# Graph edge stage on Trainium2: gathers wait for their own indices, run eight steps ahead and are spread between the scatters

## The chip, the cores and the metric

The kernel runs on one core of one Trainium2 chip. The metric is the device time of one execution in microseconds (us); the median of three runs of the kernel before is 3663.58 us (3653.1 to 3665.04).

## What is computed

```python
def _L0_gnn_ref(m, row, col, vals):            # m = layernorm(x): 50000 x 256; 25000 edges
    H = m.astype(jnp.float16)
    v = vals.astype(jnp.float16)
    msgs = H[col] * v[:, None]                 # col = dst (sorted), row = src
    return jax.ops.segment_sum(msgs, row, num_segments=N).astype(m.dtype)

x = x + _L0_gnn_ref(_layernorm(x, axis=-1), src, dst, edge_weight)
x = x + _L0_ffn_ref(_layernorm(x, axis=-1)[None], gate_w, gate_b, w1, b1, w2, b2)[0]
```

The second line is a mixture of 8 experts with a capacity limit: each of the 50000 rows is normalised, sent to the expert with the largest gate value, and passed through two matrix products there. Only the first line is touched by the change.

## The kernel before

The program has three stages, each a block of its own with a barrier at its end, so that no engine starts a stage before all have ended the last one: the **edge stage** (`edge_and_constants`), which fills a table `agg` in HBM with the sums over edges; **routing** (`route_tokens`), which reads x and `agg` in 49 steps of 1024 rows, and scatters the rows to their experts' queues; and the **experts** (`run_experts`).

The edge stage takes the 25000 edges in S = 25 steps of 1024 (`STEP`), each as G = 8 columns of 128. Step s goes like this:

- SP (`load`, L153) loads the step's indices: `dst_col`, `src_col` and `w_col` of 4 KB each, and `src_row`, the 1024 source numbers broadcast to 128 partitions (512 KB). All four raise one semaphore, `idx_loaded`, and stand in one of `INPUTS` = 3 buffers. `edge_done` counts the steps whose indices and rows are used up; SP waits for it before it writes into a buffer again.
- POOL (`gather`, L186) waits for `idx_loaded`, and for `edge_done` where its buffer of `rows` was in use, and issues 8 indirect DMAs, each of which fetches 128 rows of x into `rows` (L195).
- DVE (`body`, L296) takes the statistics of the 8 gathered tiles (`bn_stats`, L305), ACT the square root (`std`, L258) and the normalised rows (L265), DVE the masks of equal source numbers (`same`, L292; `earlier`, L334) and the weighted messages (L340). PE counts the earlier edges with the same source (L366) and sums the messages of equal sources (`ps_sum`, L376). DVE then writes `target` (L349), the row of `agg` that each sum goes to, and raises `edge_done`; ACT copies the sums out of PSUM in four parts (`sums`, L275, raising `sums_out`). ACT works in order: the square root of step s + 1 stands behind the four copies of step s.
- POOL (`scatter`, L200) waits for `edge_done` and `sums_out` of the step, and for `added` of the scatter before it, since two accumulating scatters must not be in flight together, and issues 8 accumulating indirect DMAs into `agg` (L212). `sums` and `target` have `HOLD` = 6 buffers.

POOL's order is written out by hand: gathers of steps 0 to 5, scatter(0), and from there gather(s + 5), scatter(s) by turns, in a hardware loop in the middle; the last five scatters stand alone. A number behind scatter or gather is that of its step in this text.

Before scatter(0), `agg` has to be zero. ACT issues 25 writes of 1 MB from `zeros` (L250, `zero`): 2 at once, the rest one at a time at six places of each step's body, raising `agg_zeroed`. The rest of SP's work in the stage, two loads of expert weights, follows its last index load.

Of the kernel before, what the change touches and what calls it, by code (L numbers as in the profile page):

```python
# [27 lines left out]
I32 = mybir.dt.int32  # L28
U8 = mybir.dt.uint8

P = 128
G = 8
STEP = G * P
# [23 lines left out]
HOLD = 6  # L57
INPUTS = 3
# [14 lines left out]
def edge_and_constants(nc, ctx, t):  # L73
# [22 lines left out]
    dst_col = sb("dst_col", [P, INPUTS, G], I32)  # L96
# [27 lines left out]
    agg_zeroed = sem("agg_zeroed")  # L124
    idx_loaded = [sem(f"idx_loaded{r}") for r in range(INPUTS)]
# [16 lines left out]
    AHEAD = HOLD - 1  # L142
# [6 lines left out]
    with nc.Block() as block:  # L149

        @block.sync
        def _(sp):
            def load(i, r):  # L153
                s, h = HOLD * i + r, r % INPUTS

                if not (isinstance(i, int) and s < INPUTS):
                    sp.wait_ge(edge_done, s + 1 - INPUTS)
                b = base_of(i, r)
                sp.dma_start(dst_col[:, h, :], row_view(dst[bass.ds(b, STEP)])).then_inc(idx_loaded[h], 16)
                sp.dma_start(src_col[:, h, :], row_view(src[bass.ds(b, STEP)])).then_inc(idx_loaded[h], 16)  # L160
                sp.dma_start(w_col[:, h, :], row_view(weight[bass.ds(b, STEP)])).then_inc(idx_loaded[h], 16)
                sp.dma_start(src_row[:, h, :], src[bass.ds(b, STEP)].partition_broadcast(P))\
                    .then_inc(idx_loaded[h], 16)
# [11 lines left out]
        def _(pool):  # L175
# [10 lines left out]
            def gather(i, r):  # L186
                s, h = HOLD * i + r, r % INPUTS

                pool.wait_ge(idx_loaded[h], 64 * (turn(i, r) + 1))
                pool.nop(nofuse=True)  # L190
                if not (isinstance(i, int) and s < INPUTS):
                    pool.wait_ge(edge_done, s + 1 - INPUTS)
                    pool.nop(nofuse=True)
                for c in range(G):
                    pool.indirect_dma_start(  # L195
                        out=rows[:, h, c, :], out_offset=None, in_=x[:, :],
                        in_offset=bass.IndirectOffsetOnAxis(ap=dst_col[:, h, c:c + 1], axis=0),
                    ).then_inc(gathered[h], 16)

            def scatter(i, r):  # L200
                s = HOLD * i + r
# [4 lines left out]
                if isinstance(i, int) and s == 0:  # L206
                    pool.wait_ge(agg_zeroed, 16 * ZEROS)
                else:
                    pool.wait_ge(added[r - 1], 16 * G * (i + 1 if r else i))
                    pool.nop(nofuse=True)  # L210
# [5 lines left out]

            for r in range(AHEAD):
                gather(0, r)
            gather(0, AHEAD)
            scatter(0, 0)  # L220
            for r in range(1, HOLD):
                gather(1, r - 1)
                scatter(0, r)
            with pool.Fori(1, S // HOLD - 1) as i:
                gather(i, AHEAD)
                scatter(i, 0)
                for r in range(1, HOLD):
                    gather(i + 1, r - 1)
                    scatter(i, r)
            n = S // HOLD - 1  # L230
            gather(n, AHEAD)
            scatter(n, 0)
            gather(n + 1, 0)
            for r in range(1, HOLD):
                scatter(n, r)
            scatter(n + 1, 0)
            for r in range(HOLD):
                pool.wait_ge(added[r], 16 * G * (n + (2 if r == 0 else 1)))

        @block.scalar  # L240
        def _(act):
# [9 lines left out]

            zero(0, 2 + max(0, ZEROS - AHEAD * (BANKS + 2)))

# [26 lines left out]
        def _(v):  # L280
# [15 lines left out]
            def body(i, r):  # L296
                s, h, q = HOLD * i + r, r % 2, r % INPUTS
                n = Count(s * PER + SET)
                v.wait_ge(idx_loaded[q], 64 * (turn(i, r) + 1))
# [883 lines left out]
```

## Time and profile before

| | before |
|---|---|
| median of 3 runs | 3663.58 us (3653.1 to 3665.04) |
| profiled execution: span, first to last instruction | 3533.8 us |
| the same execution's own time | not shown; the median is 129.8 us above the span |
| edge stage | 0 to about 697.5 us, barrier to 706 |
| routing | 706 to about 1310 us |
| experts | about 1310 to 3533.8 us |
| POOL busy in 105 to 600 us | 402.1 of 495 us |
| DVE, PE, ACT busy there | 260.8, 221.4, 130.2 us |
| DMA queues' share of 16 engines there | 0.45 |

A busy share counts an instruction's own time. A DMA instruction on POOL is busy while its descriptors are written; the transfer lands later, and a row on landing tells how much later. Between two instructions a profile row gives the idle time and what ended it; "issue" is idle time in which the engine waited for nothing that is shown. A wait for several semaphores is put down to the one that came last by the profile.

### The profile page before, as it was taken

Reading aid. Unit: us, or ns where it says so; the run is one execution under the profiler, and the core shown is the slowest. Engines: PE = TensorE matmul, PEld = TensorE weight load, DVE = VectorE, ACT = ScalarE, POOL = GpSimd, SP = SyncE. Lnnn points to the kernel's source line nnn. Section 1 sums busy time; section 2 is a strip of 40 time slices with the busy share of each in tenths; the row PEclk is TensorE's granted clock in tenths of the full one; section 3 lists DMA queues with packets and bytes.
Section 4 is the critical chain, followed back from the end, with each engine's and each line's share of the span. In section 5 each row is a group of like instructions: output and inputs, shape, how many; then the busy total and the mean of one; then the engine's idle time right before and its main releaser. Section 6 shows DMA issues by size and latency. Waiting matters only on the chain.

```text
span 3533.8 us, 60004 instructions
## 1 busy us (share of the span) xinstructions
PE 2919.1 (83%) x18982; PEld 2664.8 (75%) x18983; DVE 2291.9 (65%) x5804; ACT 1564.2 (44%) x2603; POOL 1796.0 (51%) x1195
## 2 busy tenths in 40 slices
PE   4544434078888876999999999999999999999998
PEld 3433434078888875988989988888988989998987
DVE  6655455077777764676676676676676676667666
ACT  2322222045555543554454555454555444454453
POOL 4788887647777773334343333434333433334332
PEclk8766666555555557999999999999999999999999
DMA  9544444399999963111111111111111121111110
GB/s 344 135 86 76 90 76 87 29 290 302 306 307 292 281 201 111 49 52 62 55 54 50 49 45 51 62 53 59 49 44 50 42 68 41 49 55 32 49 46 26
DMA packets 303467, 371.32 MB, mean 105 GB/s; under 512 B 35431, under 2 KB 263812, under 8 KB 300080
## 3 DMA queue, kind: packets, MB, share of 16 engines
q1 hardware_dynamic: 221504, 199.21, 19.2%
q0 software_dynamic: 78304, 145.23, 15.4%
q10 hardware_dynamic: 3600, 26.22, 1.8%
q8 instruction: 22, 0.36, 0.0%
q14 instruction: 37, 0.30, 0.0%
HBM read 184.33 MB, written 195.85 MB: 108 GB/s over the span
## 4 chain that ended last, share of the span: by engine, by line
PE 55%; DVE 3%; issue 2%; DVEq 1%; DMA 0%; SPq 0%; POOL 0%; ACT 0%; POOLq 0%; ACTq 0%
PE u_Y L1125 29%; PE u_H L1114 24%; PE u_T L1099 2%; DVE y L1058 1%; DVE yo L1077 1%; DVE yo L1074 0%; DVE y L1063 0%; DVE hn L1029 0%; DVE low L1068 0%; DVE hlo L1047 0%; DVE yo L1072 0%; DMA u_pay<-slots 0%; DMA slots<-blank 0%; DVEq L882 0%; DVEq L881 0%
## 5 line engine op out<-in xcount | busy, mean ns | idle before, releaser
L967 POOL DMA_INDIRECT out_x<-yo,u_token x360 | 712.3, 1979 | 1330.5 <-DVE yo L1079 1243.7
L1125 PE MATMUL u_Y<-whi,hhi 128*128 128x256 f32 x2880 | 816.0, 283 | 2.2 <-DVE hlo L1047 2.2
L999 ACT ACTIVATE hm<-u_H,b1e 128x512 f32<-128x512 f32 x720 | 496.3, 689 | 712.3 <-PE u_H L1114 684.0
L1125 PE MATMUL u_Y<-wlo,hhi 128*128 128x256 f32 x2880 | 807.2, 280 | 0.0
L1125 PE MATMUL u_Y<-whi,hlo 128*128 128x256 f32 x2880 | 806.2, 280 | 0.0
L1114 PE MATMUL u_H<-xhi,whi 128*128 128x512 f32 x1440 | 570.8, 396 | 3.1 <-DVE xlo L1036 2.5
L1114 PE MATMUL u_H<-xlo,whi 128*128 128x512 f32 x1440 | 570.3, 396 | 0.0
L1114 PE MATMUL u_H<-xhi,wlo 128*128 128x512 f32 x1440 | 570.0, 396 | 0.0
L1125 PEld LDWEIGHTS u_Y<-whi,hhi 128*128 128x128 f32 x2880 | 545.1, 189 | 2.4 <-DVE hlo L1047 2.4
L1125 PEld LDWEIGHTS u_Y<-wlo,hhi 128*128 128x128 f32 x2880 | 545.0, 189 | 0.0
L1125 PEld LDWEIGHTS u_Y<-whi,hlo 128*128 128x128 f32 x2880 | 544.3, 189 | 0.0
L534 POOL DMA_INDIRECT slots<-pay,slot_i x392 | 457.5, 1167 | 163.7 <-issue 122.5
L1058 DVE TENSOR_TENSOR y<-u_Y,b2e 128x256 f32<-128x256 f32 x360 | 127.7, 418 | 614.1 <-PE u_Y L1125 614.1
L1003 ACT ACTIVATE hhi<-hm 128x512 fp32r<-128x512 f32 x720 | 456.0, 633 | 22.9
L1047 DVE TENSOR_TENSOR hlo<-hm,hhi 128x512 fp32r<-128x512 f32 x720 | 452.7, 702 | 2.9 <-ACT hhi L1003 2.9
L212 POOL DMA_INDIRECT agg<-sums,target x200 | 328.5, 1642 | 79.2 <-issue 58.8
L599 PEld LDWEIGHTS ps_L<-gw,hT 128*128 128x128 f32 x1568 | 350.3, 332 | 0.1
L614 PE MATMUL ps_T<-ident,h 128*128 128x128 f32 x784 | 208.7, 431 | 167.3 <-ACT h L565 167.3
L599 PE MATMUL ps_L<-gw,hT 128*128 128x8 f32 x1568 | 342.4, 352 | 0.0
L1114 PEld LDWEIGHTS u_H<-xhi,whi 128*128 128x128 f32 x1440 | 271.0, 188 | 65.9 <-issue 4.1
L1114 PEld LDWEIGHTS u_H<-xhi,wlo 128*128 128x128 f32 x1440 | 270.9, 188 | 65.5
L1114 PEld LDWEIGHTS u_H<-xlo,whi 128*128 128x128 f32 x1440 | 271.0, 188 | 61.5
(127 smaller groups left out, 3757.4 us busy)
## 6 DMA issues: line engine op xcount, KB each, us to landing
xt<-in_x SPq DMA_DIRECT2D x49, 1024.0 KB
out_x<-pay SPq DMA_DIRECT2D x49, 1024.0 KB, 6.0
u_pay<-slots SPq DMA_DIRECT2D x91, 534.0 KB, 3.9
agg<-zeros ACTq DMA_DIRECT2D x25, 1024.0 KB, 10.9
at<-agg SPq DMA_DIRECT2D x49, 512.0 KB
raw<-in_L_ffn_w POOLq DMA_DIRECT2D x14, 1024.0 KB, 6.9
src_row<-in_src SPq DMA_DIRECT2D x25, 512.0 KB
slots<-pay,slot_i POOLq DMA_INDIRECT x392
```

The lines of the kernel that those rows point to most:

```text
L212: pool.indirect_dma_start(out=agg[:, :], out_offset=bass.IndirectOffsetOnAxis(ap=target[:, r, c:c + 1], axis=0), in_=sums[:, r, c, :], in_ ...
L534: pool.indirect_dma_start(out=slots[:, :], out_offset=bass.IndirectOffsetOnAxis(ap=slot_i[:, r, g:g + 1], axis=0), in_=pay[:, r, g, :], in ...
L599: last = pe.matmul(logits[:, g, :], hT[:, g * KD + kd, :], gw[:, kd, :], start=(kd == 0), stop=(kd == KD - 1))
L614: last = pe.transpose(ps_T[:, n, :], h[:, q, g, kd * P:(kd + 1) * P], ident[:])
L967: pool.indirect_dma_start(out=out[:, :], out_offset=bass.IndirectOffsetOnAxis(ap=token[:, s:s + 1], axis=0), in_=yo[:, s, :], in_offset=No ...
L999: act.activation(hm[:, f, :], ps_H[:, f % 2, :], ACT.Relu, bias=b1e[:, f:f + 1])\
L1003: act.activation(hhi[:, f, :], hm[:, f, :], ACT.Copy).then_inc(hhi_ready, 1)
L1047: v.tensor_tensor(hlo[:, f, :], hm[:, f, :], hhi[:, f, :].bitcast(F32), ALU.subtract)\
L1058: last = v.tensor_tensor(y[:, s, :], ps_Y[:, s, 0:D], b2e[:], ALU.add)
L1099: last = pe.transpose(ps_T[:, k, s * P:(s + 1) * P], hn[:, s, k * P:(k + 1) * P], ident[:])
L1114: last = pe.matmul(ps_H[:, f % 2, :], w1_at(w, buf, k, f), a[:, k, :], start=(j == 0), stop=(j == len(passes) - 1))
L1125: last = pe.matmul(ps_Y[:, s, 0:D], a[:, f, cols], w2_at(w, buf, f), start=(f == 0 and j == 0), stop=(f == KF - 1 and j == 2))
```

## The change

- **Index loads apart.** `dst_col` gets `HOLD` buffers and a semaphore of its own, `dst_loaded`. SP issues step s's `dst_col` load before it waits for `edge_done`, and the other three after. A gather waits for `dst_loaded` alone and, from step `INPUTS` on, for `edge_done`; DVE waits for the other three loads.
- **Buffers.** `INPUTS` goes from 3 to 4 and `HOLD` from 6 to 8. A gather of step s now needs `edge_done` of step s - 4 instead of s - 3.
- **Order on POOL.** 64 gathers (steps 0 to 7) stand ahead of scatter(0), instead of 48. The other 136 are dealt out evenly, 5 or 6 ahead of each of the scatters 1 to 24. The hardware loop is gone; all is straight code. The other engines keep their loop, with a body of 8 steps instead of 6.
- **Zeroing.** ACT issues 12 of the 25 writes at once, and the rest at the same six places of each step.

```diff
-HOLD = 6
-INPUTS = 3
+HOLD = 8
+INPUTS = 4
...
-    dst_col = sb("dst_col", [P, INPUTS, G], I32)
+    dst_col = sb("dst_col", [P, HOLD, G], I32)
...
             def load(i, r):
                 s, h = HOLD * i + r, r % INPUTS
+                b = base_of(i, r)
+                sp.dma_start(dst_col[:, r, :], row_view(dst[bass.ds(b, STEP)])).then_inc(dst_loaded[r], 16)
                 if not (isinstance(i, int) and s < INPUTS):
                     sp.wait_ge(edge_done, s + 1 - INPUTS)
-                b = base_of(i, r)
-                sp.dma_start(dst_col[:, h, :], row_view(dst[bass.ds(b, STEP)])).then_inc(idx_loaded[h], 16)
                 sp.dma_start(src_col[:, h, :], row_view(src[bass.ds(b, STEP)])).then_inc(idx_loaded[h], 16)
...
+            def gather(s, c):
+                r, h = s % HOLD, s % INPUTS
+                if c == 0:
+                    pool.wait_ge(dst_loaded[r], 16 * (s // HOLD + 1))
+                    pool.nop(nofuse=True)
+                    if s >= INPUTS:
+
+                        pool.wait_ge(edge_done, s + 1 - INPUTS)
+                        pool.nop(nofuse=True)
+                pool.indirect_dma_start(
+                    out=rows[:, h, c, :], out_offset=None, in_=x[:, :],
+                    in_offset=bass.IndirectOffsetOnAxis(ap=dst_col[:, r, c:c + 1], axis=0),
+                ).then_inc(gathered[h], 16)
...
+            HEAD = HOLD * G
+            SPREAD = S * G - HEAD
+            for n in range(HEAD):
+                gather(n // G, n % G)
+            scatter(0)
+            for s in range(1, S):
+
+                for n in range(HEAD + SPREAD * (s - 1) // (S - 1), HEAD + SPREAD * s // (S - 1)):
+                    gather(n // G, n % G)
+                scatter(s)
...
-            zero(0, 2 + max(0, ZEROS - AHEAD * (BANKS + 2)))
+            zero(0, ZEROS // 2)
...
-                v.wait_ge(idx_loaded[q], 64 * (turn(i, r) + 1))
+                v.wait_ge(idx_loaded[q], 48 * (turn(i, r) + 1))
```

**POOL at the start of the stage.** Each `L195` row with a wait is the first gather of a step, the `x7` behind it the other seven; `L212` is a scatter. Before, from the gathers of step 4 on:

```order
L195 DMA rows<-in_x,dst_col 128x256 [waits idx_loaded1,edge_done]
L195 DMA rows<-in_x,dst_col 128x256 x7
L195 DMA rows<-in_x,dst_col 128x256 [waits idx_loaded2,edge_done]
L195 DMA rows<-in_x,dst_col 128x256 x7
L212 DMA agg<-sums,target 51200x256 [waits edge_done,sums_out,agg_zeroed]
L212 DMA agg<-sums,target 51200x256 x7
```

and with the change, from step 4 on:

```order
L195 DMA rows<-in_x,dst_col 128x256 [waits dst_loaded4,edge_done]
L195 DMA rows<-in_x,dst_col 128x256 x7
L195 DMA rows<-in_x,dst_col 128x256 [waits dst_loaded5,edge_done]
L195 DMA rows<-in_x,dst_col 128x256 x7
L195 DMA rows<-in_x,dst_col 128x256 [waits dst_loaded6,edge_done]
L195 DMA rows<-in_x,dst_col 128x256 x7
L195 DMA rows<-in_x,dst_col 128x256 [waits dst_loaded7,edge_done]
L195 DMA rows<-in_x,dst_col 128x256 x7
L212 DMA agg<-sums,target 51200x256 [waits edge_done,sums_out,agg_zeroed]
L212 DMA agg<-sums,target 51200x256 x7
```

The gathers of steps 6 and 7 now stand ahead of scatter(0), and gather(7) waits until step 3 has used its buffers.

**POOL at the end of the stage.** Before, the last gathers and what follows them (gather(24), scatter(19), then scatter(20) to (24); the row that waits for `added5` at the top is scatter(18)):

```order
L212 DMA agg<-sums,target 51200x256 [waits edge_done,sums_out,added5]
L212 DMA agg<-sums,target 51200x256 x7
L195 DMA rows<-in_x,dst_col 128x256 [waits idx_loaded0,edge_done]
L195 DMA rows<-in_x,dst_col 128x256 x7
L212 DMA agg<-sums,target 51200x256 [waits edge_done,sums_out,added0]
L212 DMA agg<-sums,target 51200x256 x7
L212 DMA agg<-sums,target 51200x256 [waits edge_done,sums_out,added1]
L212 DMA agg<-sums,target 51200x256 x7
```

and with the change, from the gathers ahead of scatter(22), the row that waits for `added5`:

```order
L195 DMA rows<-in_x,dst_col 128x256
L195 DMA rows<-in_x,dst_col 128x256 [waits dst_loaded7,edge_done]
L195 DMA rows<-in_x,dst_col 128x256 x3
L212 DMA agg<-sums,target 51200x256 [waits edge_done,sums_out,added5]
L212 DMA agg<-sums,target 51200x256 x7
L195 DMA rows<-in_x,dst_col 128x256 x4
L195 DMA rows<-in_x,dst_col 128x256 [waits dst_loaded0,edge_done]
L195 DMA rows<-in_x,dst_col 128x256
L212 DMA agg<-sums,target 51200x256 [waits edge_done,sums_out,added6]
L212 DMA agg<-sums,target 51200x256 x7
L195 DMA rows<-in_x,dst_col 128x256 x6
L212 DMA agg<-sums,target 51200x256 [waits edge_done,sums_out,added7]
```

The first gather in this list is the last one of step 22; the row with `dst_loaded7` begins step 23, the one with `dst_loaded0` step 24. The last gathers of a step have moved from five scatters ahead of its own scatter to directly ahead of it.

## Rows read from the trace of the kernel before

**Rows 1.** Routing stage: busy us and count of each engine, clock, DMA share, GB/s.

```profile
core 0: us, PE busy (x) PEld busy (x) DVE busy (x) ACT busy (x) POOL busy (x), PEclk, DMA share, GB/s
...
706.00:1310.00 604.00, 521.93 (x2779) 502.92 (x2779) 445.31 (x1758) 322.98 (x637) 444.52 (x383) 0.50 0.94 289
```

**Rows 2.** POOL's groups, 0 to 720 us (busy us, mean ns, idle before).

```profile
L212 POOL DMA_INDIRECT agg<-sums,target x200 | 328.5, 1642 | 79.2 <-issue 58.8 <-DMA agg<-sums,target 12.8 <-DMA agg<-zeros 7.3
L195 POOL DMA_INDIRECT rows<-in_x,dst_col x200 | 193.3, 966 | 94.4 <-issue 59.4 <-DMA src_row<-in_src 26.2 <-DVE target L349 8.4
```

**Rows 3.** POOL (start us, us, what): first gathers of steps 0, 3, 4, 5; scatter(0), (1).

```profile
7.80 1.14 POOL L195 DMA_INDIRECT rows<-in_x,dst_col  x1 [5.70 <-DMA src_row<-in_src]
...
43.21 0.94 POOL L195 DMA_INDIRECT rows<-in_x,dst_col  x1 [4.84 <-DMA src_row<-in_src]
...
68.83 0.94 POOL L195 DMA_INDIRECT rows<-in_x,dst_col  x1 [15.70 <-DMA src_row<-in_src]
...
87.50 0.94 POOL L195 DMA_INDIRECT rows<-in_x,dst_col  x1 [8.45 <-DVE target L349]
...
104.76 1.63 POOL L212 DMA_INDIRECT agg<-sums,target  x1 [7.29 <-DMA agg<-zeros]
...
130.65 1.61 POOL L212 DMA_INDIRECT agg<-sums,target  x1 [0.30 <-issue]
```

**Rows 4.** Timeline of SP, first load as steps 0, 3 end; one src_row.

```profile
34.97 0.33 SPq L159 DMA_DIRECT2D dst_col<-in_dst  x1
...
73.47 1.13 SPq L162 DMA_DIRECT2D src_row<-in_src  x1
86.83 0.35 SPq L159 DMA_DIRECT2D dst_col<-in_dst  x1
```

**Rows 5.** Statistics of step 0, its last copy of sums, standard deviation of step 1.

```profile
20.90 2.71 DVE L305 BATCH_NORM_STATS2 e_stats<-rows 128x6 f32<-128x256 f32 x8 [13.71 <-DMA rows<-in_x,dst_col]
...
43.51 0.60 ACT L275 ACTIVATE sums<-ps_sum 128x512 f16<-128x512 f32 x1 [1.15 <-PE ps_sum L376]
...
44.01 0.29 ACT L258 ACTIVATE e_std<-e_mv,eps 128x8 f32<-128x8 f32 x1
```

**Rows 6.** Landing of gathers, 40 to 56, 66 to 105, 105 to 300 us.

```profile
DMA to landing us min/median/max: 7.3/7.6/7.8
...
DMA to landing us min/median/max: 7.2/8.1/8.6
...
DMA to landing us min/median/max: 2.7/3.0/4.6
```

**Rows 7.** DMA, 40 to 100 us; then 0 to 105; last, zeroing in 80 to 105.

```profile
DMA packets 5526, 24.83 MB, mean 414 GB/s; under 512 B 1987, under 2 KB 1987, under 8 KB 3019
...
DMA packets 10074, 36.35 MB, mean 346 GB/s; under 512 B 4435, under 2 KB 4435, under 8 KB 6867
...
agg<-zeros ACTq DMA_DIRECT2D x3, 1024.0 KB, 13.0
```

**Rows 8.** Timeline of one step amid the stage, from its last gather.

```profile
181.05 0.95 POOL L195 DMA_INDIRECT rows<-in_x,dst_col  x1 [0.30 <-issue]
...
206.96 0.60 ACT L275 ACTIVATE sums<-ps_sum 128x512 f16<-128x512 f32 x1 [1.15 <-PE ps_sum L376]
```

**Rows 9.** Timeline of the end: last gather, scatter (19), last copy of sums, last scatter.

```profile
595.59 0.94 POOL L195 DMA_INDIRECT rows<-in_x,dst_col  x1 [0.30 <-issue]
...
596.84 1.62 POOL L212 DMA_INDIRECT agg<-sums,target  x1 [0.30 <-issue]
...
620.79 0.60 ACT L275 ACTIVATE sums<-ps_sum 128x512 f16<-128x512 f32 x1 [1.15 <-PE ps_sum L376]
...
695.93 1.55 POOL L212 DMA_INDIRECT agg<-sums,target  x1 [0.30 <-issue]
```

**Rows 10.** Scatters, 100 to 600 us beside DVE; then 612 to 698 alone.

```profile
L212 POOL DMA_INDIRECT agg<-sums,target x154 | 256.7, 1667 | 53.9 <-issue 46.3 <-DMA agg<-zeros 7.3 <-ACT sums L275 0.3
...
L212 POOL DMA_INDIRECT agg<-sums,target x41 | 63.4, 1547 | 23.8 <-DMA agg<-sums,target 12.8 <-issue 11.0
```

More of the change, by code:

```diff
@@ L124, in edge_and_constants @@
     agg_zeroed = sem("agg_zeroed")
+    dst_loaded = [sem(f"dst_loaded{r}") for r in range(HOLD)]
     idx_loaded = [sem(f"idx_loaded{r}") for r in range(INPUTS)]
@@ L141, in edge_and_constants @@
     PER_BANK = G // BANKS
-    AHEAD = HOLD - 1
     turn = lambda i, r: (HOLD // INPUTS) * i + r // INPUTS
@@ L184, in _, with scatter @@
                                pattern=[[-1, P]], channel_multiplier=1).then_inc(pool_set, 1)
[L186 to L192, printed above, removed]
-                    pool.nop(nofuse=True)
[L194 to L201, printed above, removed]
+            def gather(s, c):
+                r, h = s % HOLD, s % INPUTS
+                if c == 0:
+                    pool.wait_ge(dst_loaded[r], 16 * (s // HOLD + 1))
+                    pool.nop(nofuse=True)
+                    if s >= INPUTS:
[5 more added lines that the diff above has]
+                ).then_inc(gathered[h], 16)
+            def scatter(s):
+                r = s % HOLD
                 pool.wait_ge(edge_done, s + 1)
@@ L205, in scatter @@
                 pool.nop(nofuse=True)
-                if isinstance(i, int) and s == 0:
+                if s == 0:
                     pool.wait_ge(agg_zeroed, 16 * ZEROS)
                 else:
-                    pool.wait_ge(added[r - 1], 16 * G * (i + 1 if r else i))
+                    pool.wait_ge(added[(s - 1) % HOLD], 16 * G * ((s - 1) // HOLD + 1))
                     pool.nop(nofuse=True)
@@ L215, in scatter @@
                     ).then_inc(added[r], 16)
[L217 to L236, printed above, removed]
+            HEAD = HOLD * G
[7 more added lines that the diff above has]
+                scatter(s)
             for r in range(HOLD):
-                pool.wait_ge(added[r], 16 * G * (n + (2 if r == 0 else 1)))
+                pool.wait_ge(added[r], 16 * G * (S // HOLD + (r < S % HOLD)))
         @block.scalar
```

## The prediction, made before the changed kernel was run

> **What bounds the kernel now.** I read the stages first (table above): the change touches the edge stage alone, and a barrier ends it, so what that stage gains or loses is what the kernel gains or loses. In the middle of the stage POOL is the bound. Its groups [rows 2] show 200 scatters at 1.642 us and 200 gathers at 0.966 us, and about 0.30 us of "issue" behind each (118.2 us over 400, which ends when nothing but the next issue was due). A gather so costs 1.27 us. A turn of 8 gathers and 8 scatters takes 25.9 us: from scatter(1) at 130.65 [rows 3] to scatter(19) at 596.84 [rows 9] are 18 turns. With 10.15 us for the gathers, 15.75 are left for 8 scatters.
>
> Computing a step is faster than that when its rows are there: SP's first load behind step 0 starts at 34.97, behind step 3 at 86.83 [rows 4], so a step ends every 17.3 us. DVE is not full in it: ACT takes the square root of step 1 at 44.01 only behind the last copy of step 0 at 43.51 [rows 5], which sets this pace. So POOL's idle time is all that the change can move, and the groups name it: 26.2 + 8.4 + 7.3 = 41.9 us ahead of scatter(0), and 12.8 at the end, where five scatters each wait for the landing of the one before.
>
> Of the 41.9, the waits of 5.70, 4.84 and 15.70 us are for `src_row`, which a gather does not use [rows 3]. The 8.45 is put down to DVE's target, but the `edge_done` which gather(5) needs stood since step 2; its `src_row` was issued at 73.47 [rows 4]. The landing of that load, 13 us later, is the better reading. The last 7.29 is for the zeros.
>
> **The head, up to scatter(0).** The first gather waits for a 4 KB load alone. Its landing is not shown. Not below 2.7 us behind its issue at about 1 us (the fastest gather landing, [rows 6]), so 3.7; not above the 7.8 of before. I take 4.0. Four steps of gathers, 40.6 us, then run without a wait. Gather(4) to (6) need steps 0 to 2, and step k ends at about 34.8 + 17.3 k: POOL comes to them at 44.6, 54.8 and 64.9, waiting some 4 us for step 2. Gather(7) needs step 3, which ends at 86.7. Its 8 gathers take 10.15: POOL is at scatter(0) at 97.2. A step 0 that ends earlier, by up to the 3.8 us of the first gather, moves this to 93.4. The first is nearer: all gathers land in 7 to 8 us while zeroing fills the queues, against 3.0 without [rows 6], and zeroing now fills them from the first microseconds; step 0's statistics began at 20.90 [rows 5].
>
> The zeros are 25 x 1.05 = 26.2 MB. Up to 105 us all transfers together were 36.35 MB, and the rate in 40 to 100 us, when the queues were full, 414 GB/s [rows 7]. With the change 12 MB are queued at once and ACT always has more to issue. Until then come a dozen more gathers of 0.13 MB and a `src_row` of 0.5: 38.4 MB, 93 us, so the last zeros land by 96 at the latest. The two bounds meet; **scatter(0) at 97** instead of 104.76: -7.8 us, with 16 gathers more behind it: -16 x 1.27 = **-20.3**. The head gains 28.1.
>
> **Order of completion amid the stage.** Between two scatters are now 5 or 6 gathers, at least 6.3 us; the exposed wait for a landing was 12.8 / 5 = 2.6 us [rows 2], so it stays hidden. Eight buffers of `sums` and `target` suffice: the gathers are never 8 steps ahead of the scatters again. SP's `dst_col` loads come a step before their gathers need them, at the head as well: nothing. The loop that is gone cost nothing visible: the gaps are 0.30 in it and outside.
>
> **The tail.** Here the change gives back more than it won. The gathers end with the scatters: a step's rows come in just ahead of its own scatter. What lies between a step's last gather and the end of its sums can be read twice: from 181.05 + 0.95 to 206.96 + 0.60 is 25.6 us [rows 8], from 596.53 to 621.39 is 24.9 [rows 9]. I take 25.2. POOL works in order, so what it does meanwhile is what the order shows:
> - step 21: one gather, scatter(20), six gathers: 1.3 + 15.75 + 7.6 = 24.6; wait 0.6.
> - step 22: its last gather is the first of the five ahead of scatter(22); four more, 5.1; wait **20.1**.
> - step 23: two gathers behind its last, 2.5; wait **22.7**. Its last four gathers are queued behind the waiting scatter(22), so it can't start sooner.
> - step 24: nothing; wait **25.2**. Its gathers are queued behind scatter(23).
>
> Together 68.6, in place of the 12.8 of five landings: **+55.8**. Before, step 24's last gather had six scatters behind it, and its 25 us were hidden under scatter(19) and (20); that cover is gone.
>
> Scatters take 1.667 us beside DVE's work and 1.547 alone [rows 10], so computing one step costs POOL 8 x 0.12 = 1.0 us. Steps 22 to 24 are now computed while POOL waits, one or two steps are left to compute behind scatter(0) besides: two fewer under scatters, **-2**. The Trainium skill has a harder rule for this (SBUF — State Buffer, section Who interferes with whom): POOL and DVE in a two-port mode shut each other out for a whole instruction. The rows show 0.12 us per scatter. If whole blocks were the case here, the term would be larger, with the same sign.
>
> **Sum**: -7.8 - 20.3 + 55.8 - 2 = **+25.7 us**. The profiled execution's span of 3533.8 becomes 3559.5, and what lies around it, 129.8 against the median, stays: **3689.3**.
>
> **Rivals.**
> 1. *Queued zeros hold up the first gathers* (slower still). If a gather's rows come only after the 12 MB issued ahead of them, or if ACT can't issue them without stalling, step 0's statistics begin 12.6 MB / 0.414 = 30 us behind the first gather's 4, at 34 instead of 21: scatter(0) at 110, the sum 13 more, +38.7, **3702**. For it: gathers land at 7.2 to 8.6 us under zeroing. Against: a write of zeros took 13.0 us in 80 to 105 us [rows 7] while gathers still took 8.1 [rows 6]; they overtake it. The Trainium skill agrees (DMA: Bandwidth & Descriptors, section Queues, rings and completion order): a DMA engine goes round its queues packet by packet, so a backlog in one costs the others their turn, not its length.
> 2. *Routing's clock rises* (not slower). Routing runs at a granted clock of 0.50, the lower level of 1.2 GHz, with PE busy 522 of 604 us and DMA at 0.94 [rows 1]. PE's last work of the edge stage now ends some 20 us ahead of routing instead of 85. If that kept the clock at 2.4 GHz, the DMA queues would be the bound: 604 x 0.94 = 568, -36, total -10: **3653**. It decides from two fifths of the stage at the high clock, where the loss falls under 11 us. Against: the 0.50 holds for 600 us of busy PE, whatever came before.
> 3. *The chain from a step's last gather to its sums is shorter where nothing else runs* (no change). Three waits hang on it, so each microsecond off it is three off the sum; at 16.6 us instead of 25.2 the sum is zero, **3664**. For it: in the steady part the chain shares DVE's and ACT's time with nothing, but POOL and the queues are busy. Against: step 24's chain of 24.9 us [rows 9] ran with DVE and ACT idle around it as well, and most of it is work of DVE, PE and ACT, one after the other.
>
> **How the numbers follow.** Some 0.3%, 11 us, is what a measurement of this kernel can tell from no change. The first reading has 0.76, rival 1 0.13, rival 2 0.05, rival 3 0.06. Its own bounds are scatter(0) at 93 to 104 (-4 to +7), and 24.9 to 25.6 for the chain, three times (±1); a median moves by some 6 us. Range 3676 to 3708, which takes in rival 1 and leaves out both others. Slower by over 0.3%: 0.87; within: 0.07; faster: 0.06.
>
> **What would show it.** Right: first gather at about 4 us, no wait for `src_row` on POOL, scatter(0) at 93 to 98, three waits of 20, 23 and 25 us for ACT's sums ahead of scatter(22), (23) and (24), the last scatter ending at about 723, routing as long as before at a clock of 0.50. Wrong: step 0's statistics at 30 us or later (rival 1), routing under 590 us (rival 2), or last scatters with waits under 10 us.

## The result, and the profile after

| | before | changed |
|---|---|---|
| median, timed in turn on one chip (4 runs each) | 3660.99 us (3653.1 to 3665.04) | 3692.12 us (3691.47 to 3700.43) |
| ratio, 95% interval | | 1.0098 (1.0078 to 1.0117) |
| profiled execution: span | 3533.8 us | 3690.3 us |
| the same execution's own time | not shown | 3691.95 us |

The change costs 31.1 us. The forecast was 3689.3, 25.7 above the median it started from, with a range of 3676 to 3708.

The table holds a warning. Of the changed kernel the span and the time of one execution stand side by side, and only 1.7 us lie between them. So the 129.8 us that the prediction put "around the span" of before can't be that. The profile of before and its median came from chips of different speed, as the experiments show (e1, e10): on chip A (e1 to e4) before takes 3658 us; on chips B (e5 to e8) and C (e9 to e12) it takes 3533 and 3531. Which chip gave the result is not known; by its 3661 us for before it is of chip A's kind and is counted as chip A below. The first profile of before, with its span of 3533.8, is one of the second kind. Each chip was used on one occasion only, so whether the chip or the occasion makes the difference is not shown. Everything below compares kernels on one kind of chip, or chip C with the first profile.

Groups of POOL in the changed kernel on chip A, 0 to 760 us (busy us, mean ns, idle time before them and what ended it); they answer to [rows 2]:

```profile
L212 POOL DMA_INDIRECT agg<-sums,target x200 | 324.5, 1623 | 133.9 <-ACT sums L265 69.2 <-issue 64.4 <-DVE target L339 0.3
L195 POOL DMA_INDIRECT rows<-in_x,dst_col x200 | 196.0, 980 | 85.8 <-issue 63.9 <-DMA dst_col<-in_dst 21.0 <-DMA agg<-sums,target 0.6
```

The 12.8 us for the landing of scatters, the 7.3 for the zeros and the 26.2 for `src_row` are gone. In their place stand 69.2 us for ACT's copies of `sums` and 21.0 us for `dst_col`. Both are new waits. The first is the tail that was forecast; the second was forecast at nothing.

The timeline of POOL at the head of the changed kernel on chip A: first gathers of steps 0 and 3 to 7, then scatter(0), answering to [rows 3].

```profile
3.60 1.14 POOL L195 DMA_INDIRECT rows<-in_x,dst_col  x1 [1.50 <-DMA dst_col<-in_dst]
...
40.52 0.94 POOL L195 DMA_INDIRECT rows<-in_x,dst_col  x1 [6.09 <-DMA dst_col<-in_dst]
...
54.71 0.94 POOL L195 DMA_INDIRECT rows<-in_x,dst_col  x1 [4.34 <-DMA dst_col<-in_dst]
...
69.80 1.08 POOL L195 DMA_INDIRECT rows<-in_x,dst_col  x1 [5.29 <-issue]
...
85.94 0.94 POOL L195 DMA_INDIRECT rows<-in_x,dst_col  x1 [5.93 <-DMA dst_col<-in_dst]
...
99.15 0.94 POOL L195 DMA_INDIRECT rows<-in_x,dst_col  x1 [3.09 <-DMA dst_col<-in_dst]
...
110.02 1.88 POOL L212 DMA_INDIRECT agg<-sums,target  x1 [0.30 <-issue]
```

The first gather starts at 3.60, as forecast. From step 3 on each step waits again. Scatter(0) starts at 110.02 instead of the forecast 97.

The timeline of POOL at the end of the same kernel, first instructions of scatter(21) to scatter(24); it answers to [rows 9].

```profile
593.31 1.61 POOL L212 DMA_INDIRECT agg<-sums,target  x1 [4.98 <-issue]
...
635.09 1.62 POOL L212 DMA_INDIRECT agg<-sums,target  x1 [20.88 <-ACT sums L265]
...
680.10 1.62 POOL L212 DMA_INDIRECT agg<-sums,target  x1 [22.79 <-ACT sums L265]
...
727.80 1.61 POOL L212 DMA_INDIRECT agg<-sums,target  x1 [25.52 <-ACT sums L265]
```

Forecast were waits of 0.6, 20.1, 22.7 and 25.2.

### The profile page after: what moved, and what is told of

Its sections match the earlier page's. It is cut to its first block, busy times and chain, and to the rows that moved or that the text cites. A ratio compares the mean times of both kernels' runs of the same rounds, so it can differ in the third digit from the quotient of the medians.

```text
span 3690.3 us, 59901 instructions
## 1 busy us (share of the span) xinstructions
PE 2927.2 (79%) x18982; PEld 2665.3 (72%) x18983; DVE 2289.7 (62%) x5804; ACT 1561.4 (42%) x2603; POOL 1748.0 (47%) x1195
## 3 DMA queue, kind: packets, MB, share of 16 engines
q0 software_dynamic: 78304, 145.23, 14.4%
## 4 chain that ended last, share of the span: by engine, by line
PE 53%; DVE 3%; issue 2%; DVEq 0%; DMA 0%; SPq 0%; POOL 0%; ACT 0%; POOLq 0%; ACTq 0%
PE u_Y L1115 28%; PE u_H L1104 23%; PE u_T L1089 2%; DVE y L1048 1%; DVE yo L1067 1%; DVE yo L1064 0%; DVE y L1053 0%; DVE hn L1019 0%; DVE low L1058 0%; DVE hlo L1037 0%; DVE yo L1062 0%; DMA slots<-blank 0%; DMA u_pay<-slots 0%; DVEq L872 0%; DVEq L871 0%
## 5 line engine op out<-in xcount | busy, mean ns | idle before, releaser
L524 POOL DMA_INDIRECT slots<-pay,slot_i x392 | 417.5, 1065 | 316.8 <-DVE slot_i L733 200.1
L212 POOL DMA_INDIRECT agg<-sums,target x200 | 324.5, 1623 | 133.9 <-ACT sums L265 69.2
L356 PE MATMUL ps_cnt<-ones,earlier 128*128 128x1 f16 x200 | 31.2, 168 | 442.4 <-DVE earlier L324 401.2
L589 PEld LDWEIGHTS ps_L<-gw,hT 128*128 128x128 f32 x1568 | 350.1, 332 | 41.9 <-ACT hT L551 34.2
L589 PE MATMUL ps_L<-gw,hT 128*128 128x8 f32 x1568 | 344.2, 353 | 37.0 <-ACT hT L551 31.1
L356 PEld LDWEIGHTS ps_cnt<-ones,earlier 128*128 128x128 f16 x200 | 25.0, 131 | 447.8 <-DVE earlier L324 406.8
L1104 PEld LDWEIGHTS u_H<-xhi,wlo 128*128 128x128 f32 x1440 | 271.1, 188 | 65.6
```

Source lines behind the costliest of these rows:

```text
L212: pool.indirect_dma_start(out=agg[:, :], out_offset=bass.IndirectOffsetOnAxis(ap=target[:, r, c:c + 1], axis=0), in_=sums[:, r, c, :], in_ ...
L356: last = pe.matmul(ps_cnt[:, c:c + 1], earlier[:, h, c, :], ones[:, 0:1], start=(c == 0), stop=True)
L524: pool.indirect_dma_start(out=slots[:, :], out_offset=bass.IndirectOffsetOnAxis(ap=slot_i[:, r, g:g + 1], axis=0), in_=pay[:, r, g, :], in ...
L589: last = pe.matmul(logits[:, g, :], hT[:, g * KD + kd, :], gw[:, kd, :], start=(kd == 0), stop=(kd == KD - 1))
L1104: last = pe.matmul(ps_H[:, f % 2, :], w1_at(w, buf, k, f), a[:, k, :], start=(j == 0), stop=(j == len(passes) - 1))
```

## The experiments

Ratios are those of a kernel to before on the same chip, with the 95% interval. "The changed kernel" is the baseline of each diff except in e1, e8, e9 and e12, which start from before.

### e1: before, profiled on chip A

No edit.

> The kernel before, unchanged, to have a second profile of it: its first profile has a span of 3533.8 us, 127 under its median, while the changed kernel's span (3690.3) lies 1.7 us under its time. Theory A: the first profile caught a shorter routing stage (604 us against about 720 in the changed kernel's), and the timed executions have the longer one; then this profile shows a span of about 3660, a routing stage of 710 to 725 us and an edge stage of 697 us as before. Theory B: the change lengthened routing; then the span is again about 3534 and routing 604.

Measured: 3658.09 us against 3658.33, ratio 0.9999 (0.9987 to 1.0012), with a profiled span of 3661.3 and 1.6 us around it. So theory A holds: the missing 130 us lie inside the program, though its sizes were short (routing 739.4 us where 710 to 725 were expected). By stages, from the first instruction of routing on POOL and its last scatter: the edge stage ends at 714.7 (first profile 706.0), routing takes 739.4 us (621.0), and what follows 2207.2 (2206.9). Routing makes nearly all of it. These windows hold routing, of before on chip A and of the changed kernel on chip C (columns as in [rows 1]; the first ends 12 us behind routing's last scatter, the second 13 us before it, as the window of [rows 1] ends 17 us before it):

```profile
714.00:1467.00 753.00, 531.17 (x2793) 504.00 (x2793) 452.49 (x1793) 321.76 (x637) 416.17 (x397) 0.50 0.75 233
```

```profile
749.00:1352.00 603.00, 524.95 (x2793) 504.93 (x2793) 446.93 (x1766) 323.38 (x637) 446.40 (x386) 0.50 0.94 289
```

The clock is the same, PE, DVE and ACT are busy for the same time within 1.3%, and by POOL's instructions routing takes 739.4 us on chip A and 615.4 on chip C. The longest rows of waits in the first window that chip C lacks are these (us in total, times, longest; "remote" is a wait ended by a signal whose sender the profile does not name):

```profile
ACT hT L561 <- remote: 197.0, 37, 10.1
DVE lg L695 <- remote: 145.7, 24, 9.5
```

In the first profile and on chip C there are no such rows in routing; there ACT's `hT` waits for PE, 146 to 147 times, 1.9 us at the longest. So on chip A engines stop for up to 10.1 us at a time where no named engine or transfer releases them. Gaps of this label stand in the edge stage there too (five waits of DVE for "remote", 21.7 us in all, in 0 to 135 us): before's scatter(0) starts at 111.37 on chip A, after 11.68 us for the zeros, against 104.76 [rows 3].

### e2: gathers end early

```diff
-for n in range(HEAD + SPREAD * (s - 1) // (S - 1), HEAD + SPREAD * s // (S - 1)):
+for n in range(HEAD + SPREAD * min(s - 1, 19) // 19, HEAD + SPREAD * min(s, 19) // 19):
```

> The changed kernel with one thing different: the 136 spread gathers are dealt out ahead of scatters 1 to 19 instead of 1 to 24, so that the last one stands five scatters ahead of its own step's, as before. My theory (the loss is in the three waits for ACT's sums, 69.2 us, and the 5.0 us ahead of scatter(21)): they go, five landings of 2.6 us come back, 61 us less than the changed kernel, about 3631 us, and less than the kernel before by 30. Rival (the loss is at the head, or in routing): less than 15 us change, above 3675.

Measured: 3626.49 us against 3658.33, ratio 0.9907 (0.9888 to 0.9926), -31.8 us against the changed kernel's +31.1: 62.9 us less (65.6 between the two medians). POOL's groups, 0 to 760 us:

```profile
L212 POOL DMA_INDIRECT agg<-sums,target x200 | 326.7, 1633 | 72.0 <-issue 59.4 <-DMA agg<-sums,target 12.5
L195 POOL DMA_INDIRECT rows<-in_x,dst_col x200 | 198.7, 993 | 83.5 <-issue 64.3 <-DMA dst_col<-in_dst 18.9 <-DMA agg<-sums,target 0.3
```

The 69.2 us for ACT's `sums` are gone and the five landings of before are back, 12.5 us. Scatter(24) starts at 668.30, 59.5 us earlier than in the changed kernel. The head is that of the changed kernel (scatter(0) at 108.76). The tail is the cause of the loss, and the order of the spread gathers alone makes it; e5 narrows that to the last ones.

### e3: zeroing late again

```diff
-            zero(0, ZEROS // 2)
+            zero(0, 2)
```

> The changed kernel with zeroing issued as before: 2 writes at once, the rest in the steps' bodies. If the 12 writes at once hold up index loads and gathers (scatter(0) began at 109.4 us in the profile where I had forecast 97), then steps 0 to 3 now end every 17.3 us again, gathers wait less for dst_col, but the last zeros land later: scatter(0) at 98 to 105 and the kernel 4 to 11 us shorter, 3681 to 3688. If zeroing at once is a gain, scatter(0) comes at 112 or later and the time is 3695 or more.

Measured: 3712.53 us, ratio 1.0152 (1.0133 to 1.017), +54.2 where the changed kernel has +31.1. No theory had that. Scatter(0) starts at 126.96, and the wait for the zeros is only 3.30 of it. Steps 0 to 3 end at 48.8, 69.9, 91.5 and 112.6, where the changed kernel had 37.5, 64.9, 81.6 and 97.9 on this kind of chip. The tail is the same: 3.30, 21.61, 23.23 and 25.73. The steps themselves were late, for no reason that the edit gives.

### e4: index loads of the first eight steps first

```diff
+            for r in range(HOLD):
+                sp.dma_start(dst_col[:, r, :], ...).then_inc(dst_loaded[r], 16)
             steps(sp, S, HOLD, load)
```

The loop then leaves out `dst_col` in its first round.

> The changed kernel with the first eight dst_col loads issued ahead of all other index loads, so that none queues behind a src_row of 512 KB. Theory: the five waits of POOL for dst_col at the head, 21 us, and the 5.3 called issue are what made scatter(0) late; they go, scatter(0) then waits for step 3's end and comes about 10.5 us behind it, at 92 to 100 us, 9 to 17 us less: about 3679. Rival: steps 0 to 3 are themselves late (step 1 ended at 64.9 us, 27.4 behind step 0), for a reason not in the dst_col loads; then scatter(0) stays within 4 us of 109.

Measured: 3705.9 us, ratio 1.0141 (1.0116 to 1.0165), +47.6. POOL's waits for `dst_col` are gone, but the steps end at 50.3, 72.4, 93.9 and 115.0, and scatter(0) starts at 126.31. As in e3 they lie some 21 to 22 us apart instead of 17.3. e11 has the same head on chip C, instruction for instruction up to scatter(0), and its steps lie 17.3 to 17.9 apart, with scatter(0) at 106.03. So what e4 shows beyond the changed kernel belongs to chip A and not to its edit. For e3 that is likely and not shown, since its kernel ran nowhere else; e12, which also issues 2 writes at once, has steps 17 us apart on chip C. Neither settles anything about the head. The head had to be read on the other chips.

### e5: gathers end one scatter earlier

```diff
-... HEAD + SPREAD * (s - 1) // (S - 1), HEAD + SPREAD * s // (S - 1)
+... HEAD + SPREAD * min(s - 1, 23) // 23, HEAD + SPREAD * min(s, 23) // 23
```

> The changed kernel with the spread gathers dealt out ahead of scatters 1 to 23 instead of 1 to 24: one scatter's difference. Theory (a chain of 25.2 us from a step's last gather to its sums, against what POOL does meanwhile): step 23's last gather now has a whole scatter and more behind it, and step 24's has scatter(23), 15.7 us: scatter(24) waits 9.6 us, the waits ahead of scatters 22 and 23 go. Scatters end 59 us earlier than in the changed kernel, at about 683, and the time is about 3633. Rival (the spreading itself costs, in proportion): a twenty-fourth of 61 us is won, 3 us.

Measured: 3510.09 us against 3532.77 on chip B, ratio 0.9933 (0.9916 to 0.9949), -22.7. Against the +40.1 of the changed kernel (e10) that is 62.8 us for moving the end of the spread by one scatter. One wait is left in the tail, on the first instruction of scatter(24):

```profile
665.07 1.54 POOL L212 DMA_INDIRECT agg<-sums,target  x1 [10.64 <-ACT sums L265]
```

That is what the chain gives: 25.2 us less the 15.75 of scatter(23) that now runs in it is 9.5. The three long waits are the whole price, and they stand or fall together.

### e6: seven steps ahead, gathers end at scatter(22)

```diff
-            HEAD = HOLD * G
+            HEAD = 7 * G
```

The other gathers are spread over scatters 1 to 22.

> The changed kernel with seven steps of gathers ahead of scatter(0) instead of eight, and the spread ended ahead of scatter(22). Theory: POOL no longer waits for step 3 ahead of scatter(0), which starts at 95 to 100 us, when the last zeros land, with 8 gathers more behind it: a gain of 0 to 5 us over e2; two landings of 2.3 us are exposed instead of five: 7 us. Scatters end at 673 to 678, about 3617 to 3622. Rival (seven steps are too few: scatter(0) waits for zeros as long as before): 3626 as e2.

Measured: 3505.53 us, ratio 0.9924 (0.9908 to 0.9941), -27.2. Scatter(0) starts at 97.56, 4.71 of it for the zeros, and two landings of 2.49 and 2.39 are all that is exposed at the end. The expectation asked for more than the rows give. By them scatter(0) is 7.2 us earlier than at 104.76, eight gathers more lie ahead of it (-10.2), and 4.9 us of landings stand for 12.8 (-7.9): -25.3. With 7 steps ahead of scatter(0) instead of 8 the total (-27.2) is no worse than in e5 or e11: the eighth step takes 10.2 us of gathers off the rest, and scatter(0) starts 8.5 us later for it (106.03 in e11).

### e7: all zeros before the first load

```diff
-            zero(0, ZEROS // 2)
+            zero(0, ZEROS)
+            sp.wait_ge(agg_zeroed, 16 * ZEROS)
```

The wait stands ahead of SP's first load.

> The changed kernel with all 25 writes of zeros issued at once and every index load held back until they have landed, so that steps 0 to 3 are computed with quiet queues. It tells what made steps 0 to 3 take 20 us each on average in the changed kernel (37.5, 64.9, 81.6, 97.9) where the first profile of before shows 17.3, with idle time of 5 to 10 us that no engine's signal ends. Theory (traffic of the zeroing slows the engines' own supply): zeros land at 67, step 0 ends at about 96, the next three every 17.0 to 17.5 us without such gaps, scatter(0) at 158, the time about 3740. Rival (the gaps come with the program, whatever the queues do): step ends 19 to 22 us apart here too, scatter(0) at 165 or later.

Measured (2 runs): 3623.49 us on chip B, ratio 1.0255 (1.0234 to 1.0275), +90.7. The first gather starts at 69.83 after 67.72 us of waiting, the steps end at 96.3, 113.0, 129.9 and 146.9, 16.9 apart, and scatter(0) starts at 158.31, as expected. It was meant to tell why chip A's steps come late, and since chip B has no such gaps with any kernel, it could not. It does show the zeroing alone: 26.2 MB in about 67 us. And a step computes nearly as fast with quiet queues (16.9) as with full ones (17.3), so its pace is that of the engines.

### e8: the split of the index loads alone, on before

`dst_col` gets `HOLD` buffers, its own semaphore and its place ahead of the wait; all else as before.

> The kernel before with the index loads apart and nothing else: dst_col in six buffers with its own semaphore, issued ahead of the wait; order, buffers and zeroing as before. POOL's waits for src_row go (26 to 29 us), but gathers 3 to 5 still need steps 0 to 2, and scatter(0) the zeros, which are issued in the steps' bodies: if zeros bound the head, scatter(0) stays at 107 to 111 and the gain is under 4 us, 3655 to 3659. Rival (src_row was the cause of the late head): scatter(0) near 95 and 3643.

Measured: 3531.95 us against 3532.77, ratio 0.9999 (0.999 to 1.0009). POOL's groups, 0 to 760 us:

```profile
L212 POOL DMA_INDIRECT agg<-sums,target x200 | 326.6, 1633 | 96.5 <-issue 58.5 <-DMA agg<-zeros 24.8 <-DMA agg<-sums,target 12.6
L195 POOL DMA_INDIRECT rows<-in_x,dst_col x200 | 194.1, 971 | 76.4 <-issue 59.4 <-DVE target L349 15.2 <-DMA dst_col<-in_dst 1.7
```

The 26.2 us for `src_row` are gone, and the wait for the zeros has grown from 7.3 to 24.8. Scatter(0) starts at 104.73, where it started at 104.76 [rows 3]. With zeroing paced by ACT's steps the zeros decide, and POOL, there earlier, only waits longer.

### e9: zeroing at once alone, on before

```diff
-            zero(0, 2 + max(0, ZEROS - AHEAD * (BANKS + 2)))
+            zero(0, ZEROS // 2)
```

> The kernel before with 12 writes of zeros at once instead of 2, and nothing else. The zeros are then ready at about 96 us instead of 104.5; but gathers 3 to 5 wait for src_row loads, which under zeroing already take 7 to 13 us and will take longer behind a deeper backlog. Theory: POOL reaches scatter(0) at 96 to 110 by its own waits, so the gain is 0 to 8 us. Rival (the backlog holds up the loads by more than the zeros gain): slower than before by 3 us or more.

Measured: 3528.86 us against 3530.87 on chip C, ratio 0.9998 (0.9988 to 1.0008). The waits for zeros are gone, those for `src_row` are 32.9 instead of 26.2 us, and scatter(0) starts at about 101.3. The limits, zeros in e8 (104.7) and `src_row` here (101.3), lie within a few us of each other: neither part helps alone.

### e10: the changed kernel on chip C

> The changed kernel as it is, once more. The kernel before took 3658 us in one set of runs and 3533 in another, so chips differ by 3.5%, and only differences against the kernel before on the same chip can be compared; the changed kernel was +31 on the first kind. On a chip where before takes 3533 my sum, made from a profile with that span, was +25.7 with scatter(0) at 97. The e5 profile there has scatter(0) at 105 for the same head, 8 us later. So: scatter(0) at 104 to 107, three waits of 20, 23 and 25 us, scatters ending at 736 to 740, and +33 to +40 us. On a chip of the first kind: +31 again.

Measured: 3571.0 us against 3530.87, ratio 1.0119 (1.0102 to 1.0136), +40.1. That is the upper end of what was expected, and scatter(0) at 108.07 is 1 us beyond it. Its profile has no such gaps, and can be laid beside the first profile of before. It shows why the head did not gain. SP's index loads there, and how long each took to land (issues of DMA from single microseconds of the timeline: at 12.09, 18.10, 39.16, 57.06 and 74.34, the loads for steps 3 to 7; last column median us from issue to landing):

```profile
dst_col<-in_dst SPq DMA_DIRECT2D x1, 4.0 KB, 26.5
...
dst_col<-in_dst SPq DMA_DIRECT2D x1, 4.0 KB, 34.5
...
dst_col<-in_dst SPq DMA_DIRECT2D x1, 4.0 KB, 28.1
...
dst_col<-in_dst SPq DMA_DIRECT2D x1, 4.0 KB, 25.9
...
dst_col<-in_dst SPq DMA_DIRECT2D x1, 4.0 KB, 22.5
```

They land at 38.6, 52.6, 67.3, 83.0 and 96.8. The first gathers of steps 3 to 7 start 0.8 to 1.3 us behind these; scatter(0) is the last row:

```profile
39.40 1.12 POOL L195 DMA_INDIRECT rows<-in_x,dst_col  x1 [4.88 <-DMA dst_col<-in_dst]
...
53.47 0.95 POOL L195 DMA_INDIRECT rows<-in_x,dst_col  x1 [3.63 <-DVE target L339]
...
68.52 0.94 POOL L195 DMA_INDIRECT rows<-in_x,dst_col  x1 [4.83 <-issue]
...
83.78 0.97 POOL L195 DMA_INDIRECT rows<-in_x,dst_col  x1 [5.42 <-DMA dst_col<-in_dst]
...
97.66 0.96 POOL L195 DMA_INDIRECT rows<-in_x,dst_col  x1 [4.10 <-DMA dst_col<-in_dst]
...
108.07 1.78 POOL L212 DMA_INDIRECT agg<-sums,target  x1 [0.30 <-issue]
```

The `edge_done` that gather(7) needs stood since step 3 ended, at 87.6; it was forecast for 86.7. So in all five the index load is the last thing waited for, the one labelled "issue" and the one labelled DVE included, and these waits, 22.9 us together, put gather(7) at 97.66 instead of the forecast 86.7. Without them scatter(0) would not have come at 97 either: the last write of zeros, issued at 61.94, took 36.9 us and landed at 98.8. So some 9 of the 11 us are the index loads' alone.

Why a 4 KB load takes 22 to 35 us: it stands at the end of a backlog in SP's queue while ACT's zeros fill the other. Five loads in a row, `dst_col`, `src_col`, `w_col`, `src_row` and the next `dst_col`, issued at 12.09, 13.74, 15.42, 16.75 and 18.10, land in this order at 38.6, 41.8, 44.7, 49.2 and 52.6. Of the 14.0 us between the two `dst_col`, 4.5 lie at the `src_row` of 512 KB and 9.5 at three loads of 4 KB. So it is not the large load alone that holds up the small one: under zeroing each small load ahead costs some 3 us as well. With the zeros landed (e7) `dst_col` lands 0.2 us behind the `src_row` ahead of it, 3.5 us after its issue. The `src_row` of the five, and the medians over 0 to 100 us:

```profile
src_row<-in_src SPq DMA_DIRECT2D x1, 512.0 KB, 32.5
...
agg<-zeros ACTq DMA_DIRECT2D x25, 1024.0 KB, 29.2
src_row<-in_src SPq DMA_DIRECT2D x8, 512.0 KB, 22.4
rows<-in_x,dst_col POOLq DMA_INDIRECT x58, 8.1
dst_col<-in_dst SPq DMA_DIRECT2D x9, 4.0 KB, 22.5
```

The zeros' own landing went from 10.9 us (first profile, 0 to 100 us) to 29.2, and the gathers', which have a queue for themselves, only from 7.4 to 8.1. The Trainium skill (DMA: Bandwidth & Descriptors, section Queues, rings and completion order) says both halves: the queues of a DMA engine take turns, and within one queue descriptors are taken in their order. These rows agree with both; the prediction used the first half only.

The end of the stage in e10, step 24's last gather, its last copy of sums and scatter(24):

```profile
698.90 0.95 POOL L195 DMA_INDIRECT rows<-in_x,dst_col  x1 [0.30 <-issue]
...
724.17 0.60 ACT L265 ACTIVATE sums<-ps_sum 128x512 f16<-128x512 f32 x1 [1.15 <-PE ps_sum L366]
...
725.62 1.61 POOL L212 DMA_INDIRECT agg<-sums,target  x1 [25.78 <-ACT sums L265]
```

### e11: index loads first, gathers end at scatter(22)

The edits of e4 and e6's spread, with 8 steps ahead of scatter(0).

> Eight steps ahead of scatter(0) as in the changed kernel, the first eight dst_col loads issued ahead of all others, and the spread ended ahead of scatter(22). Theory: the dst_col waits were what made scatter(0) late; without them POOL reaches it 10.5 us behind step 3's end. On a chip where steps end every 17.3 us that is 97 to 100, so 8 us later than e6 less 10 for the eight gathers more: scatters end at 665 to 669, -34 to -38 us against the kernel before. Where before takes 3658, the steps themselves end late (e4: scatter(0) at 126), and the result is -20 to -30. Rival (index loads are not the cause): scatter(0) at 105 or later on the first kind of chip too, and -27.

Measured: 3502.08 us against 3530.87 on chip C, ratio 0.992 (0.9904 to 0.9937), -28.8, the lowest time of all. Scatter(0) starts at 106.03, though, not before 100: the rival's numbers came. Its reason, that index loads were not the cause, does not follow, since the edit made the steps themselves late. POOL's groups, 0 to 760 us:

```profile
L214 POOL DMA_INDIRECT agg<-sums,target x200 | 327.5, 1638 | 65.4 <-issue 59.7 <-DMA agg<-sums,target 5.0 <-ACT sums L267 0.6
L197 POOL DMA_INDIRECT rows<-in_x,dst_col x200 | 197.2, 986 | 80.5 <-issue 65.4 <-DVE target L341 13.3 <-DMA dst_col<-in_dst 1.4
```

`dst_col` costs 1.4 us now and DVE's target 13.3: POOL waits for the steps to end. These are late from the start, since step 0's `src_row` is issued at 7.93 instead of 2.37, behind the eight loads, when the queues are full already. DVE's first row shows it:

```profile
27.86 0.17 DVE L292 CAST srcf<-src_col 128x8 f32<-128x8 int32 x1 [24.45 <-DMA src_row<-in_src]
```

In e10 the same instruction ran at 7.02. Step 0 so ends at 41.9 instead of 35.9. Five and a half microseconds at SP cost twenty at DVE, since meanwhile ACT was queueing its 13 writes of zeros. Scatter(0) comes 11 us behind step 3's end, at 94.8, as the theory had it; with step 3 ending at 87.6, as in e10, that would be 99 at the zeros' landing. The eight loads placed behind `src_row` of step 0, which might give that, were not tried.

### e12: the buffers alone, on before

```diff
-HOLD = 6
-INPUTS = 3
+HOLD = 8
+INPUTS = 4
```

> The kernel before with HOLD = 8 and INPUTS = 4 and nothing else: POOL's hand-written order becomes 64 gathers, scatter(0), then gather(s + 7), scatter(s), with seven lone scatters at the end. Theory: the head takes in 16 more gathers while it waits for the zeros, which are issued in the steps' bodies as before and ready at about 105 (on a chip where before takes 3533), but POOL is at scatter(0) only behind step 3 and its src_row, at 105 to 112: -20 us of gathers later, +0 to 8 at the head, and two more exposed landings, +5: -7 to -15 us. Rival (more buffers do nothing, POOL is the bound): within 3 us of before.

Measured: 3524.9 us against 3530.87, ratio 0.9984 (0.9974 to 0.9993), -6.0. POOL's groups, 0 to 760 us:

```profile
L212 POOL DMA_INDIRECT agg<-sums,target x200 | 328.8, 1644 | 76.5 <-issue 58.8 <-DMA agg<-sums,target 17.6
L195 POOL DMA_INDIRECT rows<-in_x,dst_col x200 | 197.7, 989 | 90.5 <-issue 71.5 <-DMA src_row<-in_src 18.6 <-DMA agg<-sums,target 0.3
```

This is 1 us short of the least that was expected. 16 more gathers stand ahead of scatter(0) (-20.3), but it starts at 117.43 instead of 104.76 (+12.7), since the gathers of steps 6 and 7 wait for their `src_row` too, and more scatters stand alone at the end: seven landings, 17.6 us, against 12.8 (+4.8). That is -2.8; the stage ends 1.9 us earlier than in the first profile, and where the rest of the 6.0 comes from is not shown.

## Why the prediction was right, and where it was not

It said slower by about 26 us for the tail's sake, and the tail is the reason: e2 and e5 take it back, 62.9 and 62.8 us, and are faster than before. That the number fell within 3 us of the result is luck in part. The change itself was 31.1, so 5.4 more than forecast, and the median it was added to was 2.6 higher than that of the result. On chip C, of whose kind the profile was, the change is 40.1, which misses the 25.7 by 14.4; both lie in the range, whose bounds as differences are +12.4 and +44.4. On chip A the head's error is smaller, since before's head was late there as well, and the stage's loss of 36.1 shows up as 31.1 in the median. Laid out by its own steps, with chip C for the sizes (stage ends: scatter(24) ends at 740.2 against 697.5):

| term | forecast | measured on chip C | on chip A |
|---|---|---|---|
| scatter(0) | -7.8 (97 for 104.76) | +3.3 (108.07) | -1.4 (110.02 for 111.37) |
| 16 gathers more ahead of it | -20.3 | -20.3 (count by 1.27) | -20.3 |
| tail waits less the landings | 68.6 - 12.8 = +55.8 | 74.5 - 12.8 = +61.7 | 74.2 - 12.7 = +61.5 |
| less contention | -2 | -1.5 | -4.3 |
| sum | +25.7 | +43.2 | +35.5 |
| end of the stage | | +42.7 | +36.1 |
| median | | +40.1 | +31.1 |

The row on contention is the change of busy time in POOL's groups: 328.5 to 324.7 and 193.3 to 195.6 us on chip C, 330.5 to 324.5 and 194.3 to 196.0 on chip A.

- **The head failed at one sentence**: "SP's `dst_col` loads come a step before their gathers need them, at the head as well: nothing." They do come a step before. But a step is 17 us, and at the end of SP's backlog, with 12 MB of zeros in the other queue, they take 22 to 35 (e10). The step's limit was taken from the end of step 3, 86.7 for 87.6 measured, which was right and no longer the last thing. The term is 11 us too good. Its second bound, the zeros by 96, was 3 us too early as well (98.8): the transfers ran at 381 GB/s over 0 to 100 us, not at 414. That the index loads hold up the head is read from e10's rows; no run took their wait away with all else as it was.
- **Rival 1 was half right.** It had scatter(0) at 110 and the sum at +38.7, close to what chip C shows, but by a mechanism that did not occur: the gathers were hardly held up (8.1 us in the median, 9.7 at most), step 0's statistics began at 22.05 and not at 34, and ACT's 13 issues took 17.65 us beside the path. What was held up were the loads in SP's queue.
- **The tail was right in form and 6 us small.** The chain from a step's last gather to its sums is 24.9 us for step 24 in e10 (last gather 698.90 + 0.95, last copy 724.17 + 0.60), as read from [rows 9]. The waits are 3.57, 21.79, 23.31 and 25.78 where 0.6, 20.1, 22.7 and 25.2 were forecast; The sum had nothing for the hand-over: at scatter(24) 725.62 - 724.77 = 0.85 us lie between the last copy and POOL's start, which with a chain of 24.9 us makes the 0.6 too much there and at scatter(23). At the other two the chain was longer than 25.2: 26.0 us for step 22 and 27.2 for step 21, where DVE began on the rows only 4.4 us after the last gather had ended (1.9 at step 24). Rival 3, a shorter chain, fell with this.
- **Rival 2 fell.** The granted clock of routing is 0.50 as before (e10), though PE worked up to the end of the edge stage. Routing's scatters ran from 783.6 to 1365.2 us, 581.6 us; the first profile of before has 587.3. That is not the change's doing: with before's order of gathers e8 has 581.3 (737.7 to 1319.0).
- **"What lies around the span, 129.8, stays" was wrong.** It is 1.6 to 1.7 us; the rest was another chip. The difference of two kernels is not the same on the two kinds, +31.1 and +40.1, in the main since on chip A before's head had been late already (4.7 of the 7.7 us between the two sums; the contention row has 2.8).
- **Loss of the hardware loop, buffers, straight code**: nothing was seen of them, as said.

What stays open is the cause of chip A's gaps, why e3 and e4 had later steps at the head than the kernels beside them, and what an index load without the backlog would bring.

The split, zeroing at once and the buffers alone are worth -0.8, -2.0 and -6.0 us, the first two no different from nothing. Together, with a spread that ends in time, they give -27.2 to -28.8 on chips B and C (e6, e11) and -31.8 on chip A (e2): better than both kernels. The change had all parts of a gain, and one line in the order of the gathers gave back some 60 us.

## What to carry to other kernels

When prefetches are dealt out evenly up to the last consumer on an engine that works in order, each of the last items has its whole latency in front of its own consumer, and the next item's prefetch is queued behind that wait; end the spread as many turns early as the latency asks for (here 25 us, two scatters). A small load that others wait for inherits the backlog of its queue, small loads included, and that backlog drains slowly when another queue is filled: count its landing from there and not from its size (a queue of its own was not tried here). And before a span and a median are subtracted, make sure that they are of one chip and one occasion.

## What was not expected of the hardware

- One program took 3658 us on one chip and 3531 to 3533 on two others, at the same granted clock in routing (0.50) and with PE, DVE and ACT busy for the same time within 1.3% there. The 127 us of difference in span are idle time: 118.4 in routing, 8.7 in the edge stage, 0.3 in the experts. The waits that chip C lacks are labelled "remote" (e1).
- With full queues the issue of a DMA on SP takes 1.2 to 1.9 us instead of 0.4, in e11 up to 3.9; the instructions behind it wait as well.
- One transfer of zeros took 29.2 us to land instead of 10.9 when 13 were issued at once, while all together moved little more: 381 GB/s over 0 to 100 us against 351 before.
- Under that load 4 KB loads in SP's queue landed 2.9 to 3.5 us one behind the other, nearly as far apart as the 4.5 us of a 512 KB load (e10).
- A landing between two accumulating scatters exposes 2.4 to 2.7 us wherever nothing stands between them (e2, e6, e11, e12).
